# Layer 1 of a masked attention network: edge blocks made by GpSimd in 16-bit words, row of maxima kept in PSUM

## The chip, the cores and the metric

The kernel runs on one core of a Trainium2 chip. The metric is the device time of one execution in microseconds (us), from launch to end. One core has five instruction queues that matter here: TensorE (PE in the profile; its weight loads are PEld), VectorE (DVE), ScalarE (ACT), GpSimd (POOL) and SyncE (SP, which only issues DMAs). They meet at semaphores: an instruction waits until a counter has reached a value, and the queue behind it waits too.

## What is computed

Three attention layers over a graph of 8192 nodes with 64 features, with one dense 0/1 adjacency of 8192 x 8192. In each layer a node i scores each neighbour j with leaky_relu(u_i + v_j), sets non-neighbours to a huge negative number, takes a softmax over j and sums the features h_j by it. Cut to its core:

```
# layer 0
s = (Wh @ a1)[:, None] + (We @ a2)[None, :]
e = where(adj > 0, leaky_relu(s, 0.2), -9e15)
x = layernorm(x + elu(softmax(e, 1) @ entity + x))
# layers 1 and 2, W, L1, L2, attn of their own
e = leaky_relu(u + v.T + c, 0.2)
h = 0.2 * x + 0.8 * elu(softmax(where(adj > 0, e, NEG)) @ (h @ W))
# end
out = layernorm(x + concat([x, h1, h2]) @ mlp_w + mlp_b)
```

## The kernel before

Each layer is done in 16 blocks of 512 rows i (`NB`), and each block in 64 tiles (`NT`) of 128 neighbours j. A tile is 128 x 512: neighbours on the partitions, rows of the block along the free axis. The loops are written out, and the order of the work on each engine is the order in which its function issues it: inside a block a step t from 0 to 63, with side work hung at fixed steps by constants (`T_TURN`, `T_XOR`, `T_HIST` and so on).

One tile goes through four engines. DVE starts the scores (`start_scores`, L1156): max(ua + 0.8 v_j, cb) into one of five PSUM banks `eps`. Here `ua` (row `ub` plus the row maxima) and `cb` (the row of maxima with its sign and factor) are 128 x 512 in SBUF. PE adds the mask into the same bank (L754, two matmuls, each of 64 columns of the array). ACT takes the exponential out of PSUM into `prob` (L577). PE multiplies it with the features into the bank `acc` (L798). A bank of `eps` can be started again only when ACT has read it, five tiles later. In layers 0 and 2 a further bank `den` collects the denominators (L807); in layer 1 one feature channel is replaced so that the sums hold the denominators too, and `den` lies unused. The eighth bank, `misc`, takes all the small work.

The row maxima of block b+1 are found in block b. The adjacency is stored transposed as one byte per edge, 0x38 for "no edge" and 0 for "edge", in the buffer `nt`: two blocks in turn, each in four parts m of 128 x 8192 bytes. `make_edges` (L1004) flips a part into `edges` (two buffers in turn) with an exclusive or on 32-bit words, 128 x 2048. PE counts the edges by level of v_j (`count_edges`, L765: 16 matmuls for each m, four side by side, which land in `misc`). ACT copies the counts out (`counts_out`, L633), PE folds them (`turn_counts`, L774), DVE finds the maximum level and the row value in a chain of small operations (`head`, L1022 to L1048), PE turns them into a row (`turn_maxima`, L841), ACT copies the row out (`maxima_out`, L637), PE spreads it over the partitions into `misc` (`spread_maxima`, L846), ACT copies that to `cb` (`rows_out`, L641), and DVE adds it to `ub` (`add_u`, L1162). In the steps of block b: edges of the four parts at t = 29, 32, 40 and 41 on DVE; counts on PE at t = 35, 35, 43 and 43; fold at 47; head at 51 to 53; turned maxima at 56; spread at 57; `add_u` at 63.

The tail of block b-1 (normalisation, elu, products for the next layer) lies in block b too: sums turned at t = 8, aggregation on DVE at 13, features at 20, products at 27 and 29 on PE, the output sum on DVE at t = 35 (`tail_output`, L1121). GpSimd's queue holds for each block only the tail's DMA issues: it waits for `s_oe` (products copied out) and issues the store of `u` (L521), waits for `s_y` (L1121) and issues the store of `xin` (L524). SP's queue loads the mask parts of block b+1 (`mask_load`, L437); each load waits until PE has used up the same buffer in block b-1, and part 3 thus until block b begins.

Of the kernel before, what the change touches and what calls it, by code (L numbers as in the profile page):

```python
# [16 lines left out]
P = 128  # L17
# [22 lines left out]
EDGE_FLIP = 0x38383838  # L40
LEVELS = float(HB * LV - 2)
# [63 lines left out]
def build(nc, x, adj, ent, W0, a0, W12, lin_w, lin_b, attn, mlp_w, mlp_b, out):  # L105
    with ExitStack() as ctx:
# [92 lines left out]
        miscb = misc[:, :].bitcast(BF16)  # L199
# [30 lines left out]
        s_xor = sem("edges_made")  # L230
        s_oneh = sem("levels_on_columns")
# [73 lines left out]

        def freed(l, b, j):

            if j >= ES:
                return tile(l, b, j) - ES + 1
            last = max(i for i in range(NT) if i % ES == j)  # L310
            return tile(l, b, last) - NT + 1

# [180 lines left out]
        def _(pool):  # L493
# [37 lines left out]
            for l in range(NLAYER):  # L531
                for b in range(NB):
                    tail(l, b)
# [3 lines left out]
        def _(act):  # L537
# [60 lines left out]
            def columns_out(l, b):  # L598
                act.wait_ge(s_htt, blk(l, b) + 1)
                nc.scalar.activation(ht[0:C, :], misc[0:C, :], ACT.Copy).then_inc(s_hte, 1)  # L600

            def products_out(l, b, i):

                act.wait_ge(s_om, 4 * blk(l, b) + i + 1)
                if i < 2:
                    v = misc[:, 0:2 * WC].rearrange("p (r w) -> p r w", w=WC)
# [19 lines left out]
                elif l < 2:  # L626

                    act.wait_ge(s_ust, 16 + 16 * blk(l, b))
                    nc.scalar.activation(urow[:, :], misc[0:RT, 0:P], ACT.Copy).then_inc(s_oe, 2)

            def counts_out(l, b):
                act.wait_ge(s_hist, MV * (blk(l, b) + 1))
                nc.scalar.activation(hs[:, :], misc[:, :], ACT.Copy).then_inc(s_hse, 1)  # L633

            def maxima_out(l, b, par):
                act.wait_ge(s_mt, blk(l, b) + 1)
                nc.scalar.activation(mrow[0:3, par, :], miscb[0:3, 0:BI], ACT.Copy).then_inc(s_mte, 1)  # L637
# [18 lines left out]
            for l in range(NLAYER):  # L656
                counts_out(l, 0)
                maxima_out(l, 0, 0)
                rows_out(l, 0, 0)

                def body(b, par, head, tail):
                    for t in range(NT):
# [8 lines left out]
                        if b == 0 and l == 1 and t == T_FSUM:  # L671
                            act.wait_ge(s_fs1, 1)
                            nc.scalar.activation(acc_s[0:C, 0:P], misc[0:C, 0:P], ACT.Copy).then_inc(s_fs1e, 1)
                        if b == 0 and t == T_FSUM + 4:
                            act.wait_ge(s_fsum, l + 1)
                            nc.scalar.activation(fsum[:, :], misc[:, 0:CE], ACT.Copy).then_inc(s_fsume, 1)
# [4 lines left out]
                        if head and t == T_ROWS:  # L681
# [9 lines left out]
        def _(pe):  # L691
# [66 lines left out]
            def count_edges(l, b, m):  # L758

                n = MV * blk(l, b) + m  # L760
                pe.wait_ge(s_xor, n + 1)
                for k in range(MT // 4):
                    for s in range(4):
                        j = 4 * k + s
                        mm = nc.tensor.matmul(misc[s * HB:(s + 1) * HB, :], oneh[:, m * MT + j, :],  # L765
                                              half_block(edges[:, n % 2, :], m, j), start=(m == 0 and k == 0),
# [4 lines left out]
            def turn_counts(l, b):  # L771
                pe.wait_ge(s_hse, blk(l, b) + 1)
                for r in range(RT):
                    mm = nc.tensor.matmul(misc[:, r * HB:(r + 1) * HB], hs[:, r * P:(r + 1) * P], fold[:, :],  # L774
# [3 lines left out]
            def feature_sum(l, j):  # L778
                if l == 1:
                    mm = nc.tensor.matmul(misc[0:C, 0:P], feat[:, 1, j, 0:C], ones[:, :], start=(j == 0),  # L780
# [4 lines left out]
                mm = nc.tensor.matmul(misc[:, 0:CE], ones[:, :], feat[:, l % 2, j, :], start=(j == 0),  # L785
# [52 lines left out]
            def turn_maxima(l, b):  # L838
                pe.wait_ge(s_split, blk(l, b) + 1)
                for r in range(RT):  # L840
                    mm = nc.tensor.transpose(miscb[0:3, r * P:(r + 1) * P], parts[:, r, 0:3], identb[:, :])  # L841
                mm.then_inc(s_mt, 1)

            def spread_maxima(l, b, par):
                pe.wait_ge(s_mte, blk(l, b) + 1)
                nc.tensor.matmul(misc[:, :], onesb[:, :], mrow[:, par, :], start=True, stop=True).then_inc(s_cb, 1)  # L846

            def tail_step(l, b, t):
                if t == T_TURN:
# [4 lines left out]
                    for r in range(RT):  # L854
                        if l == 1:
                            mm = nc.tensor.matmul(misc[:, r * CE:(r + 1) * CE], acc_s[:, r * P:(r + 1) * P],
                                                  turnw[:, :], start=True, stop=True)
                            continue
                        nc.tensor.matmul(misc[:, r * CE:r * CE + C], acc_s[:, r * P:(r + 1) * P], halves[:, 0:C],  # L859
                                         start=True, stop=True)  # L860
                        mm = nc.tensor.matmul(misc[:, r * CE + C:(r + 1) * CE], den_s[:, r * P:(r + 1) * P],  # L861
                                              halves[:, C:CE], start=True, stop=True)
                    mm.then_inc(s_gt, 1)
                if t == T_HT:
                    for r in range(RT):
                        mm = nc.tensor.transpose(misc[0:C, r * P:(r + 1) * P], hn[:, r, :], ident[:, :])  # L866
# [426 lines left out]
```

## Time and profile before

| what | value |
|---|---|
| median of 3 runs | 3498.52 us (3497.92 to 3498.54) |
| the profiled execution | 3499.27 us, of which the span from first to last instruction is 3497.5 us |
| busy share of the span | PE 92%, DVE 82%, ACT 65%, POOL 3% |
| mean granted TensorE clock | 0.983 |
| layer 0 | to about 1412 us; reads the 268 MB adjacency, DMA share 1.00 |
| layer 1 | about 1412 to 2380 us; 16 blocks, of which 14 in the middle follow each other at 56.9 us |
| layer 2 | about 2440 us to the end |

"Busy" is the time in which at least one instruction of the engine runs; matmul ends are modelled. A timeline row merges neighbours of one kind: start, length of the whole row, engine, line, operation, output<-inputs, shapes and count. "[1.01 <-ACT prob L577]" says that the engine sat idle for 1.01 us before it, until that line of ACT let it go.

### The profile page before, as it was taken

How to read it: one execution, taken by the hardware profiler on the slowest of the kernel's cores; microseconds unless marked ns; L12 is line 12 of the kernel's file. 1: busy time of each engine (PE TensorE's matmuls, PEld its weight loads, DVE VectorE, ACT ScalarE, POOL GpSimd, SP SyncE). 2: the span in 40 equal slices, each digit the busy share in tenths (PEclk: the TensorE clock that was granted, in tenths of full speed). 3: DMA queues.
4: the chain of work that ended last, by engine and by line, in shares of the span. 5: the costliest groups of instructions: out<-in, count | busy, mean ns of one | idle time of the engine just before them, and what ended most of it. 6: DMA issues, size and time to landing. Idle time of an engine off the chain costs nothing. (4 is left out here: it accounts for less than half of the span.)

```text
span 3497.5 us, 58252 instructions
## 1 busy us (share of the span) xinstructions
PE 3203.8 (92%) x22959; PEld 1152.7 (33%) x22959; DVE 2873.2 (82%) x5283; ACT 2269.0 (65%) x3933; POOL 114.3 (3%) x138
## 2 busy tenths in 40 slices
PE   1679999999999999799999999988999999999998
PEld 0323333333333333333333333334333333333333
DVE  5468888888888875699999999986888888888886
ACT  0247766676776666377777787773666666666665
POOL 0000000000000000000000000000000000000000
PEclk9989999999999999899999999998999999999999
DMA  8999999999999951222222222112111211221210
GB/s 253 283 348 346 341 329 347 336 333 340 343 333 341 333 180 54 85 85 97 76 100 73 100 73 101 72 61 85 69 72 64 90 71 57 86 82 57 85 33 7
DMA packets 414116, 578.71 MB, mean 165 GB/s; under 512 B 294402, under 2 KB 315010, under 8 KB 389266
## 3 DMA queue, kind: packets, MB, share of 16 engines
q1 hardware_dynamic: 409458, 564.40, 50.2%
q0 software_dynamic: 4384, 10.59, 1.0%
q8 instruction: 180, 2.95, 0.4%
q14 instruction: 94, 0.77, 0.1%
HBM read 430.10 MB, written 77.69 MB: 145 GB/s over the span
## 5 line engine op out<-in xcount | busy, mean ns | idle before, releaser
L1156 DVE SCALAR_TENSOR_TENSOR eps<-ua,v8col,cb 128x512 f32<-128x512 f32 x2800 | 1971.3, 754 | 376.3 <-ACT prob L577 238.9
L577 ACT ACTIVATE prob<-eps,v2col 128x512 f32<-128x512 f32 x2560 | 1628.4, 688 | 692.2 <-PE eps L754 678.9
L798 PE MATMUL acc<-prob,feat 128*64 128x512 f32 x5120 | 1303.3, 605 | 6.6 <-ACT acc_s L585 6.6
L754 PE MATMUL eps<-nt,nbig 128*64 128x512 fp8e4 (+2 forms) x6542 | 994.3, 384 | 114.4 <-DVE eps L1156 110.4
L754 PEld LDWEIGHTS eps<-nt,nbig 128*64 128x64 bf16 (+2 forms) x6542 | 329.8, 104 | 956.0 <-DVE eps L1156 612.5
L798 PEld LDWEIGHTS acc<-prob,feat 128*64 128x64 f32 x5120 | 326.2, 137 | 397.9 <-issue 215.0
L577 ACT ACTIVATE mi<-eps,v2col 128x512 f32<-128x512 f32 x512 | 328.0, 686 | 156.7 <-PE eps L754 152.7
L995 DVE TENSOR_SCALAR mi<-stage 128x1024 uint8<-128x1024 int32 x512 | 352.2, 689 | 62.9 <-DMA stage<-in_adj_dram 62.5
L807 PE MATMUL den<-prob,ones 128*32 128x512 f32 x3072 | 397.0, 604 | 0.0
L798 PE MATMUL acc<-mi,feat 128*64 128x512 f32 x1024 | 264.8, 597 | 0.0
L1004 DVE TENSOR_SCALAR edges<-nt 128x2048 int32<-128x2048 int32 x192 | 234.2, 1220 | 31.1 <-PE misc L765 16.3
L765 PE MATMUL misc<-edges,oneh 128*32 128x512 fp8e4 x3072 | 190.8, 390 | 70.6 <-DVE edges L1004 55.8
L564 ACT ACTIVATE eps<-ub,v8col 128x512 f32<-128x512 f32 x272 | 189.4, 696 | 0.0
L807 PEld LDWEIGHTS den<-prob,ones 128*32 128x32 f32 x3072 | 67.1, 108 | 301.0 <-issue 301.0
L765 PEld LDWEIGHTS misc<-edges,oneh 128*32 128x32 bf16 x3072 | 85.0, 98 | 198.3 <-issue 81.1
L807 PE MATMUL den<-mi,ones 128*32 128x512 f32 x1024 | 123.1, 598 | 0.0
L751 PE MATMUL eps<-mrow,onesb 128*32 128x512 bf16 (+1 forms) x800 | 106.5, 379 | 0.0
L633 ACT ACTIVATE hs<-misc 128x512 f32<-128x512 f32 x48 | 28.3, 589 | 93.8 <-PE misc L765 93.8
L798 PEld LDWEIGHTS acc<-mi,feat 128*64 128x64 f32 x1024 | 68.2, 137 | 54.4 <-issue 20.2
L878 PEld LDWEIGHTS misc<-wcat,ht 65*128 65x128 f32 x384 | 52.5, 198 | 77.8 <-issue 49.5
L637 ACT ACTIVATE mrow<-misc 3x512 bf16<-3x512 bf16 x48 | 28.1, 586 | 76.3 <-PE misc L841 76.3
L878 PE MATMUL misc<-wcat,ht 65*128 65x130 f32 (+1 forms) x384 | 69.8, 306 | 6.5 <-ACT pj L624 4.5
(159 smaller groups left out, 1407.1 us busy)
## 6 DMA issues: line engine op xcount, KB each, us to landing
stage<-in_adj_dram SPq DMA_DIRECT2D x512, 512.0 KB, 6.5
nt<-nt_d SPq DMA_DIRECT2D x128, 1024.0 KB, 5.2
nt_d<-nt SPq DMA_DIRECT2D x64, 1024.0 KB, 7.2
ub<-u_d SPq DMA_DIRECT2D x48, 256.0 KB, 5.2
xy_d<-xin POOLq DMA_DIRECT2D x32, 256.0 KB, 3.3
xin<-xy_d SPq DMA_DIRECT2D x32, 256.0 KB, 2.9
nt<-mi SPq DMA_TRANSPOSE x256, 7.2
xin<-in_x_dram SPq DMA_DIRECT2D x16, 128.0 KB, 6.3
```

The lines of the kernel that those rows point to most:

```text
L564: nc.scalar.activation(eps[:, j % ES, :], ub[:, par, :], ACT.Relu, bias=v8col[:, j:j + 1], scale=1.0 - ALPHA).then_inc(s_filla, 1)
L577: nc.scalar.activation(weights(l, j), eps[:, j % ES, :], ACT.Exp, bias=v2col[:, j:j + 1]).then_inc(s_p, 1)
L633: nc.scalar.activation(hs[:, :], misc[:, :], ACT.Copy).then_inc(s_hse, 1)
L751: nc.tensor.matmul(et[c:c + cols, :], onesb[:, c:c + cols], mrow[:, par, :], start=False, stop=False, skip_group_check=True, tile_position ...
L754: mm = nc.tensor.matmul(et[c:c + cols, :], nbig[:, c:c + cols], edge, start=False, stop=True, skip_group_check=True, tile_position=(0, c))
L765: mm = nc.tensor.matmul(misc[s * HB:(s + 1) * HB, :], oneh[:, m * MT + j, :], half_block(edges[:, n % 2, :], m, j), start=(m == 0 and k == 0),
L798: mm = nc.tensor.matmul(acc[h:h + C, :], feat[:, l % 2, j, 0:C], weights(l, j), start=(k == 0), stop=(k == NT // 2 - 1))
L807: mm = nc.tensor.matmul(den[32 * i:32 * i + 32, :], ones[:, 0:32], weights(l, QUAD * k + i), start=(k == 0), stop=(k == NT // QUAD - 1))
L878: mm = nc.tensor.matmul(misc[:, r * WC + w:(r + 1) * WC], ht[:, (2 * i + r) * P:(2 * i + r + 1) * P], wcat[:, l, w:WC], start=True, stop=True)
L995: dv.tensor_scalar(out, src, 0, ONE8, ALU.is_le, ALU.mult).then_inc(s_mask, 1)
L1004: dv.tensor_scalar(edges[:, n % 2, :].bitcast(I32), nt[:, b % 2, m, :].bitcast(I32), EDGE_FLIP, None, ALU.bitwise_xor).then_inc(s_xor, 1)
L1156: dv.scalar_tensor_tensor(eps[:, j % ES, :], ua[:, par, :], v8col[:, j:j + 1], cb[:, par, :], ALU.add, ALU.max).then_inc(s_fill, 1)
```

## The change

It touches layer 1 only, in four ways.

- `make_edges` for blocks 1 to 15 of layer 1 leaves DVE's queue and goes to GpSimd's. The 32-bit exclusive or becomes multiply by -1 and add 0x3838 on 16-bit words, in four instructions of 128 x 1024 words for each part m. So GpSimd gets 16 such instructions for each block. Block 0's edges stay on DVE.
- The edge buffers of parts 2 and 3 are new ones, laid over `mi`, which is idle in layer 1 (`edges1`); parts 0 and 1 keep `edges`.
- GpSimd's queue in block b is now: parts 0 and 1 of block b+1, the tail of block b-1 with its two waits and two DMA issues, parts 2 and 3 of block b+1. PE's `count_edges` waits for GpSimd's semaphore `s_edge`.
- In layer 1 the copy of the maxima row to `cb` on ACT (`rows_out`) is gone. The row stays in the PSUM bank where PE spread it, and `start_scores` and `add_u` read it there. `misc` and `den` change roles from block to block: one holds the row of the running block, the other takes the small work.

```diff
+        edges1 = mi[:, :, :].rearrange("p s w -> p (s w)").rearrange("p (m w) -> p m w", m=2)
...
+        def max_bank(b):
+
+            return (misc, den)[b % 2][:, :]
+
+        def work_bank(l, b):
+
+            return max_bank(b + 1) if l == 1 else misc[:, :]
+
+        def by_pool(l, b):
+            return l == 1 and b > 0
+
+        def edge_buffer(l, b, m):
+
+            return edges1[:, m - 2, :] if by_pool(l, b) and m >= 2 else edges[:, m % 2, :]
...
-            for l in range(NLAYER):
-                for b in range(NB):
-                    tail(l, b)
+            def make_edges(b, m):
+
+                n = MV * blk(1, b) + m
+                sl, count = landed(1, b, m)
+                pool.wait_ge(sl, count)
+                if b > 1:
+                    pool.wait_ge(s_hist, n - MV + 1)
+                elif m < 2:
+                    pool.wait_ge(s_hist, n - 1)
+                w = MT * BI // EDGE_PARTS
+                for i in range(EDGE_PARTS):
+                    nc.gpsimd.tensor_scalar(edge_buffer(1, b, m)[:, i * w:(i + 1) * w].bitcast(U16),
+                                            nt[:, b % 2, m, i * w:(i + 1) * w].bitcast(U16), -1.0,
+                                            float(EDGE_FLIP & 0xffff), ALU.mult, ALU.add).then_inc(s_edge, 1)
+
+            for b in range(NB):
+                tail(0, b)
+            for b in range(NB):
+                for m in range(MV if b < NB - 1 else 0):
+                    make_edges(b + 1, m)
+                    if m == 1 and b > 0:
+                        tail(1, b - 1)
+            tail(1, NB - 2)
+            tail(1, NB - 1)
+            for b in range(NB):
+                tail(2, b)
...
-                        if head and t == T_ROWS:
+                        if head and t == T_ROWS and l != 1:
                             rows_out(l, b + 1, 1 - par)
...
-                pe.wait_ge(s_xor, n + 1)
+                if by_pool(l, b):
+                    pe.wait_ge(s_edge, EDGE_PARTS * (MV * (b - 1) + m + 1))
+                else:
+                    pe.wait_ge(s_xor, MV * (NB + 1 + b if l == 2 else blk(l, b)) + m + 1)
...
-                dv.scalar_tensor_tensor(eps[:, j % ES, :], ua[:, par, :], v8col[:, j:j + 1], cb[:, par, :],
+                dv.scalar_tensor_tensor(eps[:, j % ES, :], ua[:, par, :], v8col[:, j:j + 1], maxima(l, b, par),
                                         ALU.add, ALU.max).then_inc(s_fill, 1)
...
-                            for m in range(MV):
+                            for m in range(0 if by_pool(l, b + 1) else MV):
                                 if t == T_XOR[m]:
                                     make_edges(l, b + 1, m)
```

The other edits of the diff replace `misc` by `work_bank(...)` where PE, ACT and DVE use the small-work bank.

## Rows read from the trace of the kernel before

**Rows 1.** Busy time by stretch: one middle block of layer 1, then block 0 of it.

```profile
core 0: us, PE busy (x) PEld busy (x) DVE busy (x) ACT busy (x) POOL busy (x), PEclk, DMA share, GB/s
1899.50:1956.40 56.90, 53.45 (x342) 19.10 (x338) 54.02 (x97) 44.02 (x78) 1.30 (x2) 1.00 0.25 88
1428.80:1501.20 72.40, 68.35 (x417) 31.49 (x419) 53.00 (x83) 41.30 (x66) 0.00 (x0) 0.95 0.13 44
```

**Rows 2.** Who waited for whom in that block: us in total, times, longest.

```profile
PEld eps L754 <- DVE eps L1156: 18.3, 33, 1.7
...
DVE eps L1156 <- ACT prob L577: 2.2, 3, 1.0
```

**Rows 3.** Timeline of DVE through that block.

```profile
1899.49 0.69 DVE L1162 SCALAR_TENSOR_TENSOR ua<-ub,cb 128x512 f32<-128x512 f32 x1
1900.21 9.37 DVE L1156 SCALAR_TENSOR_TENSOR eps<-ua,v8col,cb 128x512 f32<-128x512 f32 x14
...
1926.16 1.22 DVE L1004 TENSOR_SCALAR edges<-nt 128x2048 int32<-128x2048 int32 x1
1927.30 2.07 DVE L1156 SCALAR_TENSOR_TENSOR eps<-ua,v8col,cb 128x512 f32<-128x512 f32 x3
1929.29 0.41 DVE L1121 TENSOR_TENSOR xin<-xin,pj 128x256 f32<-128x256 f32 x1
...
1941.61 0.76 DVE L1156 SCALAR_TENSOR_TENSOR eps<-ua,v8col,cb 128x512 f32<-128x512 f32 x1 [1.01 <-ACT prob L577]
...
1944.19 0.29 DVE L1022 TENSOR_SCALAR he<-misc 128x128 int32<-128x128 int32 x1
...
1948.68 0.17 DVE L1048 CAST parts<-nm 128x4 bf16<-128x4 f32 x1
...
1956.36 0.69 DVE L1162 SCALAR_TENSOR_TENSOR ua<-ub,cb 128x512 f32<-128x512 f32 x1
```

**Rows 4.** Timeline of PE in the same block.

```profile
1930.79 1.91 PE L765 MATMUL misc<-edges,oneh 128*32 128x512 fp8e4 x32
1932.63 0.62 PE L754 MATMUL eps<-nt,nbig 128*64 128x512 fp8e4 x4
...
1933.94 0.60 PE L754 MATMUL eps<-nt,nbig 128*64 128x512 fp8e4 x4
...
1938.54 1.91 PE L765 MATMUL misc<-edges,oneh 128*32 128x512 fp8e4 x32
```

**Rows 5.** Groups of instructions in layer 1, 1480 to 2380 us: count, busy, mean ns, idle before.

```profile
L1071 DVE SCALAR_TENSOR_TENSOR g<-fsum,emp,misc 128x65 f32<-128x65 f32 x64 | 13.6, 275 | 4.9 <-PE misc L856 4.9
...
L641 ACT ACTIVATE cb<-misc 128x512 f32<-128x512 f32 x15 | 9.0, 597 | 7.5 <-PE misc L846 7.5
...
L1022 DVE TENSOR_SCALAR he<-misc 128x128 int32<-128x128 int32 x16 | 4.7, 291 | 4.3 <-PE misc L774 2.9
...
L1024 DVE TENSOR_TENSOR hx<-hx,he 128x128 f32<-128x128 f32 x15 | 4.4, 293 | 0.5
```

**Rows 6.** Timeline of GpSimd in the same block.

```profile
1930.00 0.78 POOL L524 DMA_DIRECT2D xy_d<-xin  x1 [0.44 <-DVE xin L1121]
```

**Rows 7.** All of GpSimd's instructions by form, whole span: busy, mean ns.

```profile
L527 POOL TENSOR_TENSOR rstd<-mom,half 128x4 f32<-128x4 f32 x16 | 23.0, 1435 | 1053.3 <-DVE mom L1060 1053.3
...
L499 POOL MEMSET mrow<- 128x1024 bf16 x1 | 1.0, 951 | 0.1
...
L506 POOL TENSOR_SCALAR_AFFINE_SELECT halves<-halves 128x64 f32<-128x64 f32 x2 | 0.5, 238 | 0.1
...
L502 POOL TENSOR_SCALAR_AFFINE_SELECT identb<-identb 128x128 bf16<-128x128 bf16 x1 | 0.3, 290 | 0.0
...
L499 POOL MEMSET ident<- 128x128 f32 x1 | 0.2, 204 | 0.1
```

**Rows 8.** Timeline of SP's queue in the same block.

```profile
1933.16 24.13 SPq L437 DMA_DIRECT2D nt<-nt_d  x4
```

**Rows 9.** Line 1156 over the whole span: duration ns min/median/max.

```profile
L1156 DVE SCALAR_TENSOR_TENSOR eps<-ua,v8col,cb x2800: 728/754/762, 125.5 to 3469.9; 128x512 f32<-128x512 f32 x187
```

More of the change, by code:

```diff
@@ L230, in build @@
         s_xor = sem("edges_made")
+        s_edge = sem("edges_made_by_pool")
         s_oneh = sem("levels_on_columns")
@@ L599, in columns_out @@
                 act.wait_ge(s_htt, blk(l, b) + 1)
-                nc.scalar.activation(ht[0:C, :], misc[0:C, :], ACT.Copy).then_inc(s_hte, 1)
+                nc.scalar.activation(ht[0:C, :], work_bank(l, b + 1)[0:C, :], ACT.Copy).then_inc(s_hte, 1)
             def products_out(l, b, i):
@@ L764, in count_edges @@
                         j = 4 * k + s
-                        mm = nc.tensor.matmul(misc[s * HB:(s + 1) * HB, :], oneh[:, m * MT + j, :],
-                                              half_block(edges[:, n % 2, :], m, j), start=(m == 0 and k == 0),
+                        mm = nc.tensor.matmul(wb[s * HB:(s + 1) * HB, :], oneh[:, m * MT + j, :],
+                                              half_block(eb, m, j), start=(m == 0 and k == 0),
                                               stop=(m == MV - 1 and k == MT // 4 - 1), skip_group_check=True,
@@ L773, in turn_counts @@
                 for r in range(RT):
-                    mm = nc.tensor.matmul(misc[:, r * HB:(r + 1) * HB], hs[:, r * P:(r + 1) * P], fold[:, :],
+                    mm = nc.tensor.matmul(work_bank(l, b - 1)[:, r * HB:(r + 1) * HB], hs[:, r * P:(r + 1) * P], fold[:, :],
                                           start=True, stop=True)
@@ L779, in feature_sum @@
                 if l == 1:
-                    mm = nc.tensor.matmul(misc[0:C, 0:P], feat[:, 1, j, 0:C], ones[:, :], start=(j == 0),
+                    mm = nc.tensor.matmul(work_bank(1, 0)[0:C, 0:P], feat[:, 1, j, 0:C], ones[:, :], start=(j == 0),
                                           stop=(j == NT - 1))
@@ L784, in feature_sum @@
                     return
-                mm = nc.tensor.matmul(misc[:, 0:CE], ones[:, :], feat[:, l % 2, j, :], start=(j == 0),
+                mm = nc.tensor.matmul(work_bank(l, 0)[:, 0:CE], ones[:, :], feat[:, l % 2, j, :], start=(j == 0),
                                       stop=(j == NT - 1))
@@ L840, in turn_maxima @@
                 for r in range(RT):
-                    mm = nc.tensor.transpose(miscb[0:3, r * P:(r + 1) * P], parts[:, r, 0:3], identb[:, :])
+                    mm = nc.tensor.transpose(work_bank(l, b - 1).bitcast(BF16)[0:3, r * P:(r + 1) * P], parts[:, r, 0:3], identb[:, :])
                 mm.then_inc(s_mt, 1)
@@ L845, in spread_maxima @@
                 pe.wait_ge(s_mte, blk(l, b) + 1)
-                nc.tensor.matmul(misc[:, :], onesb[:, :], mrow[:, par, :], start=True, stop=True).then_inc(s_cb, 1)
+                nc.tensor.matmul(work_bank(l, b - 1), onesb[:, :], mrow[:, par, :], start=True, stop=True).then_inc(s_cb, 1)
             def tail_step(l, b, t):
+                wb = work_bank(l, b + 1)
                 if t == T_TURN:
@@ L877, in tail_step @@
                             w = C if l == 0 else 0
-                            mm = nc.tensor.matmul(misc[:, r * WC + w:(r + 1) * WC],
+                            mm = nc.tensor.matmul(wb[:, r * WC + w:(r + 1) * WC],
                                                   ht[:, (2 * i + r) * P:(2 * i + r + 1) * P], wcat[:, l, w:WC],
@@ L921, in body @@
                         if b == 0 and t < (NT + 2) // 3:
-                            if t == 0:
-                                pe.wait_ge(s_cbe, blk(l, 0) + 1)
+                            if t == 0 and l != 1:
+                                pe.wait_ge(s_cbe, copied(l, 0))
                             for j in range(3 * t, min(3 * t + 3, NT)):
@@ L927, in body @@
                             pe.wait_ge(s_fs1e, 1)
-                            nc.tensor.matmul(misc[:, 0:CE], acc_s[0:C, 0:P], turnw[0:C, :], start=True,
+                            nc.tensor.matmul(work_bank(1, 0)[:, 0:CE], acc_s[0:C, 0:P], turnw[0:C, :], start=True,
                                              stop=True).then_inc(s_fsum, 1)
@@ L1148, in tail_step, with maxima @@
                     tail_result(b)
+            def maxima(l, b, par):
+                return max_bank(b) if l == 1 else cb[:, par, :]
             def start_scores(l, b, j, par):
```

46 lines of the change are left out of this document (27 added, 19 removed).

## The prediction

> **What bounds the kernel now.** The change touches layer 1 alone, so I read that layer and nothing of the whole span. I cut one middle block out of it with the view of busy time by stretch [rows 1]: 56.9 us, DVE busy 54.02 (95%), PE 53.45, ACT 44.02, GpSimd 1.30. Two engines are close to full, so the next question is who waits for whom [rows 2]: in the block PE's weight loads wait 18.3 us for DVE's line 1156, while DVE waits 2.2 us for ACT. DVE sets the pace and PE follows closely behind. The timeline of DVE [rows 3] gives the price of a tile: 14 starts of scores in 9.37 us are (9.37 - 0.75)/13 = 0.663 us from start to start. The timeline of PE [rows 4] gives PE's price where it isn't waiting: 1933.94 - 1932.63 = 1.31 us for two tiles, 0.655 us each. The engines differ by 1% on the plain tile; what side work each has beside its 64 tiles, and where, decides. Block 0 of layer 1 is another case: 72.4 us with PE busy 68.35 and DVE 53.00 [rows 1], bound by PE.
>
> **What leaves DVE.** Four edge instructions for each block. Each takes 1.22 us, and the next start of scores comes 1927.30 - 1926.16 = 1.14 us after it began [rows 3]: 4 x 1.14 = 4.56 us of 56.9. Block 0 loses them too, but there DVE is not the bound, so I count nothing. Blocks 1 to 14 make the edges of the next block: 14 blocks gain at most 14 x 4.56 = 64 us.
>
> **What comes up behind it.** PE's two pairs of counts stand at t = 35 and 43 and take 1932.63 - 1930.79 = 1.84 us each [rows 4]; with the fold at 47, some 0.9 us, PE has about 4.6 us of side work between t = 35 and 47. Until now DVE had its edges in the same stretch and the two cancelled. Afterwards DVE has only the output sum there, 0.3 us (1929.29 to about 1929.6, rows 3 with its three starts before). DVE can run about four tiles ahead on five banks, 4 x 0.66 = 2.6 us. What is left, 4.6 - 0.3 - 2.6 = 1.7 us, becomes a wait of DVE for ACT, where it waits some 1.3 us today (1.01 of it in one place [rows 3]). By DVE's sum a block is 56.9 - 4.56 + 0.4 = 52.7 us. PE's busy time of 53.45 us [rows 1] stands against that; a part of it is modelled matmul tails while it waits, so it is not a hard floor, but I take it as the nearer limit: a gain of 56.9 - 53.45 = 3.4 us.
>
> **The copy of the row that goes.** ACT loses one instruction of 597 ns in each block [rows 5]. ACT is busy 44.02 of 56.9 us [rows 1], so this is worth nothing by itself. The path from the spread row to `add_u` is 0.6 us shorter, but `add_u` stands at the block's last step and shows no idle time before it [rows 3]. Nothing, once 0.6 us at the layer's start. The turn of the two banks costs no instruction: the wait of the small work in the bank of the old row is already met, since that block's last start of scores is eight steps past when t = 8 comes.
>
> **The maxima read from PSUM.** 64 starts for each block now read one operand in PSUM and write PSUM. No row of before shows that pair. The nearest rows [rows 5]: line 1022 reads 128 x 128 from PSUM in 291 ns and line 1024 does as much from SBUF alone in 293 ns; line 1071 reads 65 elements from PSUM beside an SBUF operand in 275 ns. So I take zero. Bounds: minus 0.01 us, and above by line 1071: 275 ns less 65 elements at 1.04 ns leaves 207 ns fixed, against 754 - 533 = 221 ns at line 1156 [rows 9]; these rows give no positive end, and I leave 0.03 us as room, 64 x 0.03 = 1.9 us a block.
>
> A rule speaks against this. The Trainium skill, "VectorE: DVE Perf Modes", section "The TRN2 errata — SBUF-src ops pay a fixed extra latency per instruction", gives VectorE 58 cycles of fixed cost with an SBUF source and 120 with a PSUM source. By it each start would be some 65 ns longer, 4.1 us a block, and the gain would be gone. The rows of 128 x 128 here, 291 against 293 ns, don't agree with it.
>
> **GpSimd's price.** The trace has no GpSimd instruction that streams 1024 words in and out. What it has [rows 7]: a memset of 128 x 1024 in 951 ns and of 128 x 128 in 204 ns, so 747/896 = 0.83 ns for an element; a select with input and output of 128 x 64 in 238 and of 128 x 128 in 290 ns, 0.81 ns for an element and 186 ns fixed. By that slope 1024 words take 186 + 1024 x 0.83 = 1.04 us. Upper bound: two arithmetic operations and the conversion from and to 16 bits could cost a second pass, 0.19 + 2 x 0.85 = 1.9 us (estimate). Lower bound: 0.95 us. The power of 128 x 4 at 1435 ns shows that this engine's software can be far slower than its elements, so the upper end isn't far-fetched. I take 1.0 us from start to start, nearest to the select, which also reads and writes. In all 16 x 1.0 = 16 us of a block of which GpSimd uses 1.3: room enough. The order is what matters.
>
> **The wait that is added.** PE's counts wait for `s_edge`, and behind that wait stands all of PE: masks, products, then ACT and DVE. For parts 0 and 1 there is no danger: their masks are issued in SP's queue from 1933.16 [rows 8], in the block before, and GpSimd makes them right after parts 2 and 3, some 25 us or more before t = 35 of the next block. Parts 2 and 3 are late by construction: GpSimd's queue has the tail before them, which waits for `s_y` (line 1121 on DVE, t = 35), and then issues a DMA of 0.78 us that ends at 1930.78 [rows 6]. PE's first pair of counts starts at 1930.79, the second at 1938.54 [rows 4]: 7.75 us, and part 3 is wanted 0.9 us later. In a shorter block this becomes 1.84 + 8 x 0.655 = 7.1 us, 8.0 us for part 3. Eight instructions of 1.0 us take 8.0 us. It just fits; GpSimd gains a little since DVE reaches t = 35 up to 1 us earlier against PE. I charge 0.4 us a block. The two issues of DMA aren't delayed: parts 0 and 1 have been done long before. The loads of SP depend on PE's masks, as before.
>
> **The sum.** 3.4 - 0.4 = 3.0 us for each of 14 blocks, 42 us. Made against the profiled execution (3499.27 us, span 3497.5) this gives 3457; the median of the runs lies 0.75 us below that execution, so 3456.5 us.
>
> **Rivals.**
>
> A, GpSimd blocks DVE. Parts 0 and 1 of the block after next run right behind parts 2 and 3, from about 8 to 16 us after the first counts. DVE's chain of row maxima lies at 1944.19 to 1948.85, 13.4 to 18 us after them [rows 3, 4], a little earlier in a shorter block: it would run against some four GpSimd instructions. If a GpSimd instruction holds something that the chain's two-operand instructions need, about three of them wait 0.8 us each: 2.4 us, DVE's sum 55.1 us, gain 1.8 x 14 = 25 us, 3473 us. If all four are waited for in full, 4 us, the gain is nearly gone, 3495. For: nothing in the trace. Against: line 1156 has two SBUF operands and never takes more than 762 ns [rows 9], also while GpSimd computes its power in layers 0 and 2, though that touches only 4 elements. The Trainium skill, "SBUF — State Buffer", section "Who interferes with whom", says just this: a VectorE instruction with two SBUF inputs, or in a two-port mode, and a GpSimd instruction that reads SBUF exclude each other for their whole length. By it the starts of scores, with one SBUF input left, would be safe, and the chain would pay.
>
> B, GpSimd is slower than 1.5 us an instruction, and the kernel gets slower. Then PE stands at part 3's wait, at t = 43 of every block. At 1.7 us part 3 is late by 8 x 1.7 - 8.0 = 5.6 us, and DVE's sum is 52.7 + 5.6 = 58.3 us, 1.4 more than now: 14 x 1.4 = 20 us, 3518 us. It decides from 8T - 8.0 = 4.2, T = 1.53 us. At the upper bound of 1.9 us it would be 3540 us. For: no row of such an instruction, and the 1435 ns. Against: the slope of 0.8 ns for an element with input and output.
>
> C, a start of scores costs more with PSUM on both sides. DVE's sum has 56.9 - 52.7 = 4.2 us to lose, so from 4.2/64 = 0.066 us for each start the gain is gone: 3498 us, no change, and slower beyond. Against: the 291 ns row.
>
> D, the edges come off DVE and the time stays, because PE's chain is the true bound at today's pace. Against: PE waits 18.3 us for DVE in a block [rows 2]. Within 0.2%.
>
> **How the numbers follow.** Chances: the sum 0.45; A 0.22 (0.04 of it no change); B 0.22 (0.18 slower, 0.04 no change); C 0.07 (half no change, half slower); D 0.04. Differences below 0.2%, 7 us, can't be told from none. So faster 0.63, no change 0.15, slower 0.22. Low end: DVE's full 4.56 us for 14 blocks gives 3435. High end: B at 1.7 us, 3518, with what lies above it left out.
>
> **What would show it.** The block in layer 1 should be 53.9 us, against 52.7 by DVE alone. GpSimd's edge instructions 1.0 to 1.05 us. Line 1156 at 754 ns and 0.663 us from start to start; 0.73 would be C. PE's idle time at the counts should be under 1 us a block in place of the waits for line 1156; several us there, released by GpSimd, are B. Lines 1022 to 1048 on DVE should still take 4.7 us from first to last; 7 us or more, or instructions of 0.3 us that take 1 us, are A. Layers 0 and 2 should keep their lengths to 1 us. Wrong above all would be the one price that no row carries: that of a GpSimd instruction on 1024 16-bit words.

## The result

The changed kernel takes 3533.7 us (median of 5 executions, 3518.0 to 3534.5), the kernel before 3497.9 us beside it; the ratio is 1.009, interval 1.0078 to 1.0103. It is slower by 36 us, where 42 us less were forecast. The profiled execution took 3534.2 us, with a span of 3532.3 us.

The page of the changed kernel, busy time and two groups of GpSimd (busy, mean ns, idle before):

```profile
PE 3203.6 (91%) x22848; PEld 1160.9 (33%) x22959; DVE 2839.7 (80%) x5223; ACT 2265.7 (64%) x3917; POOL 366.1 (10%) x378
...
L563 POOL TENSOR_SCALAR edges<-nt 128x1024 uint16<-128x1024 uint16 x120 | 125.6, 1047 | 64.0 <-PE den L814 41.4
...
L563 POOL TENSOR_SCALAR mi<-nt 128x1024 uint16<-128x1024 uint16 x120 | 125.5, 1046 | 9.5
```

GpSimd went from 3% to 10% of the span, DVE from 2873.2 to 2839.7 us: 60 edge instructions are gone, 73 us, but more than half of that has come back, most of it (some 29 us) in the chain of row maxima, as the rows below show. The clock differs from execution to execution: the four of 3529.8 to 3534.5 us ran at a mean granted clock of 0.974 to 0.976, the one of 3518.0 us at 0.983, as before the change.

A block of layer 1 from `add_u` to `add_u` was 56.87 us [rows 3]. Of the same 14 blocks the first 13 now take between 58.6 and 60.5 us, mostly 59.1 and 60.2 us in turn, 59.55 us on average; the 14th takes 57.1 us. The timeline of one of them on DVE, with waits:

```profile
1980.51 0.68 DVE L1219 SCALAR_TENSOR_TENSOR ua<-ub,den 128x512 f32<-128x512 f32 x1
...
2008.69 0.76 DVE L1210 SCALAR_TENSOR_TENSOR eps<-ua,v8col,den 128x512 f32<-128x512 f32 x1 [0.67 <-ACT prob L621]
...
2014.90 5.37 DVE L1210 SCALAR_TENSOR_TENSOR eps<-ua,v8col,den 128x512 f32<-128x512 f32 x8 [1.83 <-ACT prob L621]
2022.42 0.75 DVE L1210 SCALAR_TENSOR_TENSOR eps<-ua,v8col,den 128x512 f32<-128x512 f32 x1 [2.15 <-ACT prob L621]
...
2025.01 0.29 DVE L1072 TENSOR_SCALAR he<-misc 128x128 int32<-128x128 int32 x1
2025.34 0.60 DVE L1073 SCALAR_TENSOR_TENSOR hx<-he,kstep 128x128 f32<-128x128 int32 x1
2025.97 1.09 DVE L1074 TENSOR_TENSOR hx<-hx,he 128x128 f32<-128x128 f32 x1
2027.09 0.29 DVE L1075 TENSOR_REDUCE kmax<-hx 128x4 f32<-128x128 f32 x1
2027.41 0.66 DVE L1076 TENSOR_SCALAR emp<-kmax 128x4 f32<-128x4 f32 x1
2027.98 0.28 DVE L1077 TENSOR_SCALAR vm<-kmax,gst 128x4 f32<-128x4 f32 x1
2028.29 0.89 DVE L1080 SCALAR_TENSOR_TENSOR ns<-vm,gst,vucol 128x4 f32<-128x4 f32 x1
...
2031.74 0.17 DVE L1098 CAST parts<-nm 128x4 bf16<-128x4 f32 x1
...
2039.71 0.68 DVE L1219 SCALAR_TENSOR_TENSOR ua<-ub,misc 128x512 f32<-128x512 f32 x1
```

Three things stand in it. The four edge instructions are gone, and in their place DVE waits for ACT: 0.67, 1.83 and 2.15 us are the longest waits. The chain of row maxima, which began 44.7 us into the block [rows 3], begins after 44.5 us: 4.56 us of work have left DVE's queue and the chain has come 0.2 us forward. And the chain itself, 4.66 us from line 1022 to 1048 [rows 3], takes 6.9 us: its small instructions of 0.17 to 0.3 us take 0.60, 1.09, 0.66 and 0.89 us. GpSimd beside it:

```profile
2010.38 0.78 POOL L545 DMA_DIRECT2D xy_d<-xin  x1
2011.24 8.93 POOL L563 TENSOR_SCALAR mi<-nt 128x1024 uint16<-128x1024 uint16 x8
2020.24 8.93 POOL L563 TENSOR_SCALAR edges<-nt 128x1024 uint16<-128x1024 uint16 x8
```

It works without a pause from 2011.24 to 2029.17, and the last instruction of the chain that is long starts at 2028.29. Everything after that has its old length. Not all of the long ones have two operands in SBUF: line 1076, with one SBUF input and a constant, takes 0.66 us in place of 0.17, while line 1077, with one SBUF input and two scalars read from SBUF, keeps its 0.28 us. The same block by stretch, first the kernel before and then the changed one: to the first counts, to the chain, the chain, to the next `add_u`.

```profile
core 0: us, PE busy (x) PEld busy (x) DVE busy (x) ACT busy (x) POOL busy (x), PEclk, DMA share, GB/s
1899.50:1930.80 31.30, 29.50 (x169) 10.58 (x166) 31.13 (x54) 26.75 (x50) 1.30 (x2) 1.00 0.13 43
1930.80:1944.20 13.40, 13.14 (x123) 5.32 (x122) 11.99 (x18) 8.34 (x14) 0.00 (x0) 1.00 0.59 208
1944.20:1948.80 4.60, 3.47 (x20) 1.14 (x20) 4.19 (x17) 3.21 (x5) 0.00 (x0) 1.00 0.46 194
1948.80:1956.40 7.60, 7.34 (x41) 2.06 (x37) 6.72 (x12) 5.71 (x10) 0.00 (x0) 1.00 0.00 0
```

```profile
1980.50:2011.80 31.30, 29.87 (x169) 10.97 (x165) 29.85 (x54) 27.23 (x50) 1.91 (x3) 1.00 0.12 44
2011.80:2025.00 13.20, 12.98 (x123) 5.32 (x122) 8.80 (x13) 8.37 (x14) 12.25 (x13) 1.00 0.58 209
2025.00:2031.90 6.90, 3.52 (x18) 1.06 (x18) 6.48 (x17) 3.22 (x5) 3.94 (x4) 0.97 0.32 132
2031.90:2039.70 7.80, 7.64 (x34) 2.42 (x33) 6.68 (x11) 4.95 (x8) 0.00 (x0) 0.81 0.00 1
```

The first two stretches have nearly kept their length although DVE does 1.3 and 3.2 us less in them: PE is busy 13.14 of 13.4 us and 12.98 of 13.2 us in the second. The third is 2.3 us longer. The fourth, in which nothing was added and a copy was taken from ACT, is 0.2 us longer too, and there the granted clock is 0.81 in place of 1.00.

The changed kernel holds a control of its own: the 14th block. GpSimd has made the last edges before its chain begins. Its chain and the stretch behind it:

```profile
2323.41:2328.05 4.64, 3.52 (x20) 1.13 (x20) 4.22 (x17) 3.22 (x5) 0.00 (x0) 1.00 0.00 0
2328.05:2334.67 6.62, 6.21 (x32) 1.79 (x31) 6.58 (x11) 4.97 (x8) 0.00 (x0) 1.00 0.00 0
```

Without GpSimd beside it the chain takes 4.64 us again, and the clock stays at 1.00.

PE's timeline shows where the clock can have fallen; it pauses 2.72 us, then 0.66 us, while DVE is in the chain:

```profile
2026.67 1.03 PE L847 MATMUL acc<-prob,feat 128*64 128x512 f32 x4
2030.42 0.41 PE L799 MATMUL eps<-nt,nbig 128*64 128x512 fp8e4 x2 [2.72 <-DVE eps L1210]
2031.49 0.64 PE L799 MATMUL eps<-nt,nbig 128*64 128x512 fp8e4 x2 [0.66 <-DVE eps L1210]
2031.91 1.91 PE L847 MATMUL acc<-prob,feat 128*64 128x512 f32 x4
```

The next four products take 1.91 us in place of 1.03.

From these I formed theory H: the edges were hidden behind PE; what costs is that GpSimd excludes DVE's two-operand instructions, and that PE's pause during the chain lets its clock fall. The words "two-operand" are too narrow: line 1076 has one.

### The profile page after: what moved, and what is told of

It is laid out like the page before. It is cut to its first block and busy times, and to the rows that moved or that the text cites. A ratio compares the mean times of both kernels' runs of the same rounds, so it can differ in the third digit from the quotient of the medians.

```text
span 3532.3 us, 58303 instructions
## 1 busy us (share of the span) xinstructions
PE 3203.6 (91%) x22848; PEld 1160.9 (33%) x22959; DVE 2839.7 (80%) x5223; ACT 2265.7 (64%) x3917; POOL 366.1 (10%) x378
## 5 line engine op out<-in xcount | busy, mean ns | idle before, releaser
L1210 DVE SCALAR_TENSOR_TENSOR eps<-ua,v8col,cb 128x512 f32<-128x512 f32 x1776 | 1269.7, 755 | 323.6 <-ACT prob L621 188.5
L847 PE MATMUL acc<-prob,feat 128*64 128x512 f32 x5120 | 1320.6, 612 | 7.0 <-ACT acc_s L629 7.0
L1210 DVE SCALAR_TENSOR_TENSOR eps<-ua,v8col,misc 128x512 f32<-128x512 f32 x512 | 349.8, 751 | 72.4 <-ACT prob L621 71.3
L1210 DVE SCALAR_TENSOR_TENSOR eps<-ua,v8col,den 128x512 f32<-128x512 f32 x512 | 347.7, 750 | 50.0 <-ACT prob L621 49.1
L814 PE MATMUL misc<-edges,oneh 128*32 128x512 fp8e4 x2336 | 147.6, 395 | 71.2 <-DVE edges L1054 56.3
L1054 DVE TENSOR_SCALAR edges<-nt 128x2048 int32<-128x2048 int32 x132 | 161.2, 1221 | 30.5 <-PE misc L814 16.6
L538 POOL TENSOR_TENSOR rstd<-mom,half 128x4 f32<-128x4 f32 x16 | 23.1, 1446 | 1096.3 <-DVE mom L1110 1096.3
L563 POOL TENSOR_SCALAR edges<-nt 128x1024 uint16<-128x1024 uint16 x120 | 125.6, 1047 | 64.0 <-PE den L814 41.4
L548 POOL TENSOR_TENSOR rstd<-mom,half 128x4 f32<-128x4 f32 x16 | 23.0, 1438 | 1051.0 <-DVE mom L1110 1051.0
L563 POOL TENSOR_SCALAR mi<-nt 128x1024 uint16<-128x1024 uint16 x120 | 125.5, 1046 | 9.5
L814 PEld LDWEIGHTS misc<-edges,oneh 128*32 128x32 bf16 x2336 | 67.7, 99 | 166.1 <-issue 64.2
```

Source lines behind the costliest of these rows:

```text
L563: nc.gpsimd.tensor_scalar(edge_buffer(1, b, m)[:, i * w:(i + 1) * w].bitcast(U16), nt[:, b % 2, m, i * w:(i + 1) * w].bitcast(U16), -1.0, ...
L814: mm = nc.tensor.matmul(wb[s * HB:(s + 1) * HB, :], oneh[:, m * MT + j, :], half_block(eb, m, j), start=(m == 0 and k == 0), stop=(m == MV ...
L847: mm = nc.tensor.matmul(acc[h:h + C, :], feat[:, l % 2, j, 0:C], weights(l, j), start=(k == 0), stop=(k == NT // 2 - 1))
L1054: dv.tensor_scalar(edge_buffer(l, b, m).bitcast(I32), nt[:, b % 2, m, :].bitcast(I32), EDGE_FLIP, None, ALU.bitwise_xor).then_inc(s_xor, 1)
L1210: dv.scalar_tensor_tensor(eps[:, j % ES, :], ua[:, par, :], v8col[:, j:j + 1], maxima(l, b, par), ALU.add, ALU.max).then_inc(s_fill, 1)
```

## The experiments

Ratios are against the kernel before on the same chip. A block is one in the middle of layer 1. The diffs show the edit that matters, not always all of it. Layer 0 is the same in all kernels, and yet the first `add_u` of layer 1 lies between 1428.6 and 1440.2 us in the profiled executions, so the length of a block is the surer measure.

**The edges off DVE, nothing in their place.**

```diff
-                            for m in range(MV):
+                            for m in range(0 if l == 1 else MV):
                                 if t == T_XOR[m]:
                                     make_edges(l, b + 1, m)
...
```

The constant buffer that PE counts is filled once by GpSimd.

> The kernel before, with DVE's 60 edge instructions of blocks 1 to 15 of layer 1 left out and nothing put in their place: PE counts a constant buffer, so the row maxima are those over all nodes and part of layer 1's result is not the reference's. Theory P (the prediction's step: the edges stand on DVE's path): a block of 53.5 us in place of 56.9, the kernel at 3440 to 3457 us. Theory H (the edges lay in a stretch, t = 24 to 47, that PE bounds anyway, and were hidden behind it): a block of 56.4 to 56.7 us, the kernel at 3490 to 3496 us, and DVE idle for some 4 us more in each block, released by ACT.

Measured: 3492.9 us, ratio 0.9983 (0.9973 to 0.9992), a block of 56.23 us, a little under the range of theory H, which holds against P. DVE's waits in the kernel without edges:

```profile
1933.34 5.40 DVE L1166 SCALAR_TENSOR_TENSOR eps<-ua,v8col,cb 128x512 f32<-128x512 f32 x8 [1.75 <-ACT prob L583]
1940.46 0.76 DVE L1166 SCALAR_TENSOR_TENSOR eps<-ua,v8col,cb 128x512 f32<-128x512 f32 x1 [1.72 <-ACT prob L583]
...
1955.20 0.68 DVE L1172 SCALAR_TENSOR_TENSOR ua<-ub,cb 128x512 f32<-128x512 f32 x1
```

DVE waits 5.7 us in this block in place of 2.2 [rows 2]: of the 4.56 us, 3.5 became waits for ACT, which waits for PE, 0.64 became gain, and the remaining 0.4 us is not accounted for. Fourteen blocks would gain 9 us; the median shows 6.3 us, with an interval from 3 to 9.

**The row in PSUM, edges on DVE.**

```diff
         def by_pool(l, b):
-            return l == 1 and b > 0
+            return False
...
```

GpSimd's queue and PE's wait for the edges are put back as they were before the change.

> The changed kernel with the edges back on DVE: what is left of the change is the row of maxima in PSUM and the two banks in turn. If the PSUM operand is free, 3496 to 3499 us, with line 1156's successor at 750 to 755 ns. If it costs 65 ns for each start of scores, a block of 59 us or more and 3530 us or more, which by itself would be the whole loss of the changed kernel.

Measured: 3484.9 us, ratio 0.9960 (0.9945 to 0.9975), a block of 55.91 us. The operand is free, and more: this half of the change gains 0.96 us a block, and the expectation had nothing of that. ACT's timeline of the kernel before, at the block's end, and the groups of starts in the new kernel:

```profile
1952.16 0.59 ACT L637 ACTIVATE mrow<-misc 3x512 bf16<-3x512 bf16 x1 [0.80 <-PE misc L841]
...
1953.82 0.60 ACT L641 ACTIVATE cb<-misc 128x512 f32<-128x512 f32 x1 [0.50 <-PE misc L846]
1954.31 3.57 ACT L577 ACTIVATE prob<-eps,v2col 128x512 f32<-128x512 f32 x6
```

```profile
L1205 DVE SCALAR_TENSOR_TENSOR eps<-ua,v8col,den 128x512 f32<-128x512 f32 x512 | 347.4, 748 | 12.6 <-ACT prob L616 11.8
L1205 DVE SCALAR_TENSOR_TENSOR eps<-ua,v8col,misc 128x512 f32<-128x512 f32 x470 | 319.7, 750 | 12.7 <-ACT prob L616 11.9
```

Before, two copies of 0.6 us stood close together on ACT, and the exponentials behind them came late to DVE: in the block of [rows 3], DVE's starts wait 0.88 us for ACT at 1955.03. Without the second copy that wait is gone, and the stretch from the chain to `add_u` takes 6.62 us in place of 7.51. ACT was busy 44 of 56.9 us [rows 1] and still late at that one place. The starts take 748 and 750 ns with one operand in PSUM, 754 before [rows 9].

**GpSimd waits for the chain.**

```diff
                 pool.wait_ge(sl, count)
+                if m == 0:
+                    pool.wait_ge(s_split, blk(1, b - 1) + 1)
```

> The changed kernel with one wait more on GpSimd: part 0 of the next block's edges is not begun before DVE's chain of row maxima is done. Theory H with exclusion (GpSimd blocks the chain's two-operand instructions, 2.2 us a block, and PE's pause there lets its clock fall): the chain back from 6.9 to 4.7 us, no stretches at half clock, a block of 56.6 to 57.0 us, 3494 to 3500 us. Rival L (part 3 late at PE, 0.3 us, and the late counts cost the time): unchanged, 3515 to 3535 us.

Measured: 3481.4 us, ratio 0.9948 (0.9933 to 0.9962), a block of 55.75 us. One wait more on GpSimd turns a loss of 36 us into a gain of 18 us. It is even better than expected, by about what the row in PSUM brings. The chain's stretch and the one behind it:

```profile
1934.10:1938.70 4.60, 3.47 (x20) 1.13 (x20) 4.18 (x17) 3.22 (x5) 0.00 (x0) 1.00 0.47 196
1938.70:1945.40 6.70, 6.29 (x36) 1.82 (x35) 6.67 (x12) 4.96 (x8) 6.11 (x6) 1.00 0.00 0
```

The chain takes 4.6 us again and the clock stays at 1.00. GpSimd works now in the fourth stretch, 6.11 of 6.7 us, where DVE has only starts with one SBUF operand and `add_u`.

**A quarter of the counting.**

```diff
-                for k in range(MT // 4):
+                for k in range(1 if l == 1 and b > 0 else MT // 4):
```

> The kernel before, with edges on DVE, but PE does a quarter of the counting matmuls in blocks 1 to 15 of layer 1 (16 of 64 for each block), so part of layer 1's result is not the reference's. It takes 2.8 us of PE's work out of each block's stretch t = 35 to 47. Theory H (PE bounds that stretch): now DVE's edges come to the front; 1 to 2.5 us a block less, 3465 to 3485 us. Theory P (DVE bounds it): 0 to 0.3 us a block, 3493 to 3498 us.

Measured: 3479.9 us, ratio 0.9945 (0.9930 to 0.9959), a block of 55.57 us. It is the counterpart of the first experiment: in the same stretch 2.8 us less on PE gain 1.3 us a block, while 4.56 us less on DVE gained 0.64. PE was the nearer bound there, and DVE's edges were close behind.

**The row back in SBUF, edges on GpSimd.**

```diff
-                return max_bank(b) if l == 1 else cb[:, par, :]
+                return cb[:, par, :]
```

with the copy on ACT and its waits put back.

> The changed kernel with the row of maxima copied to SBUF and read there by the starts of scores, so that these have two SBUF operands again; GpSimd still makes the edges. Theory X (a GpSimd instruction and a VectorE instruction with two SBUF operands exclude each other): starts beside GpSimd's 16 instructions wait for up to 1 us each, some 10 to 16 us a block, the kernel at 3650 to 3780 us, with starts of scores of 1.5 us and more in the trace. Rival (only the chain's small instructions suffer): 3545 to 3555 us, that is the changed kernel plus the 14 us of the copy.

Measured: 3614.0 us, ratio 1.0331 (1.0310 to 1.0352), a block of 64.85 us. DVE beside GpSimd's work:

```profile
1984.90 3.40 DVE L1209 SCALAR_TENSOR_TENSOR eps<-ua,v8col,cb 128x512 f32<-128x512 f32 x5
...
1991.82 5.02 DVE L1209 SCALAR_TENSOR_TENSOR eps<-ua,v8col,cb 128x512 f32<-128x512 f32 x5
1997.03 15.67 DVE L1209 SCALAR_TENSOR_TENSOR eps<-ua,v8col,cb 128x512 f32<-128x512 f32 x11 [0.19 <-ACT prob L621]
```

Eleven starts take 15.67 us, 1.42 us each in place of 0.66: each waits for the GpSimd instruction that runs, and GpSimd for each start (its mean went from 1.05 to 1.28 and 1.37 us). So theory X holds in kind. I had expected 3650 to 3780 us, too much; that the starts that run at this pace are fewer and that a part of the delay falls where PE bounds is my guess. Against the 3534 us with the row in PSUM the difference is 80 us, of which the copy on ACT is some 13. What the copy costs without GpSimd beside it shows in the 14th block, where GpSimd has no edges left: the chain takes 4.65 us and the stretch behind it 7.51 us, as before the change, against 6.62 without the copy.

**One piece for each part.**

```diff
-EDGE_PARTS = 4
+EDGE_PARTS = 1
```

> The changed kernel with each edge part made in one GpSimd instruction of 4096 words in place of four of 1024. By theory X what counts is how long GpSimd still works when the chain begins, 44.5 us into the block, and how many gaps it leaves: one instruction takes some 3.6 us, four of them end about 45.5 us into the block, so the chain waits once, about 0.7 us, and then runs free; part 3 is in time. Block 56.0 to 56.5 us, clock without falls, kernel at 3480 to 3492 us. Rival (a longer instruction holds DVE longer, so the loss grows): 3535 us and more.

Measured: 3520.2 us, ratio 1.0063 (1.0043 to 1.0083), blocks of 57.4 to 58.8 us. Neither expectation. The chain waits once, as foreseen (a block of 57.81 us):

```profile
2017.46 0.29 DVE L1072 TENSOR_SCALAR he<-misc 128x128 int32<-128x128 int32 x1
2017.79 1.55 DVE L1073 SCALAR_TENSOR_TENSOR hx<-he,kstep 128x128 f32<-128x128 int32 x1
2019.38 0.29 DVE L1074 TENSOR_TENSOR hx<-hx,he 128x128 f32<-128x128 f32 x1
```

but for 1.3 us and not 0.7: GpSimd's four instructions take 3.6 us each, the third waits 0.54 us here for its load (from 0 to 2.1 us in others), so they end 45.8 us into the block, and the chain begins at 44.1, not 44.5. And the clock does fall, to 0.80 behind the chain, so that a delay of 1.3 us costs 2.5 us against the best kernel below. Longer instructions bring less loss here: the harm doesn't grow with the length of one instruction.

**Eight pieces for each part.**

```diff
-EDGE_PARTS = 4
+EDGE_PARTS = 8
```

> The changed kernel with each edge part in eight GpSimd instructions of 512 words. By the slope 0.70 us from start to start, 11.2 us for parts 2 and 3 in place of 8.9: part 3 is some 2.5 us late at PE, and GpSimd still works through the whole chain, so more of its instructions wait, each for less (0.3 us on average, some nine of them). Block 61 to 63 us, kernel at 3555 to 3590 us. Rival (short instructions hold DVE little, so the loss shrinks): below 3520 us.

Measured: 3557.8 us, ratio 1.0171 (1.0150 to 1.0191), blocks of 60.9 and 62.0 us. The mean of a GpSimd instruction is 0.62 us, part 3 comes late, the fold at 47.2 us in place of 43.4, and more instructions of the chain are stretched, each by less (line 1074 by 0.3 us, 1080 by 0.2, 1085 and 1093 by 0.3). The chain itself is shorter than in the changed kernel, 5.9 to 6.0 us in nearly all blocks; what makes these blocks longer is that it begins 48.3 us into them and not 44.5. So smaller pieces cost here through the late part 3, not through the chain.

**Everything before the tail.**

```diff
                 pool.wait_ge(sl, count)
+                if m == 0:
+                    pool.wait_ge(s_split, blk(1, b - 1) + 1)
+                if m == 2 and b > 1:
+                    pool.wait_ge(s_h, blk(1, b - 1))
...
-                    if m == 1 and b > 0:
+                    if m == 3 and b > 0:
                         tail(1, b - 1)
```

> The changed kernel with GpSimd's order changed: parts 0 and 1 only when the chain of row maxima is done, parts 2 and 3 only when DVE has finished the features of the tail (t = 20), and all four before the tail's two DMA issues. So GpSimd works beside no two-operand instruction of DVE and no part is late. Expected: the gain of the row in PSUM (0.96 us a block) and of the edges (0.64 us) together, a block of 55.3 us, the kernel at 3469 to 3476 us. If the gain of the two doesn't add up: 3478 to 3485 us, as with the wait for the chain alone.

Measured: 3475.4 us, ratio 0.9936 (0.9920 to 0.9953), a block of 55.36 us: the fastest kernel of the study, 23 us under the one before. GpSimd's timeline:

```profile
1960.81 8.93 POOL L567 TENSOR_SCALAR mi<-nt 128x1024 uint16<-128x1024 uint16 x8 [15.39 <-issue]
1972.26 0.56 POOL L542 DMA_DIRECT2D u_d<-urow  x1 [2.52 <-ACT urow L677]
...
1991.86 8.92 POOL L567 TENSOR_SCALAR edges<-nt 128x1024 uint16<-128x1024 uint16 x8 [18.25 <-DVE parts L1102]
```

Parts 2 and 3 end 2.5 us before the tail's store has to go out. The two gains add up: 0.96 + 0.64 = 1.60 us, and 56.87 - 55.36 = 1.51 us. Against the wait for the chain alone, 55.75 - 55.36 = 0.39 us is what the late part 3 cost.

**The chain made longer, without GpSimd beside it.**

```diff
+                for i in range(7 if by_pool(l, b) else 0):
+                    step(dv.tensor_reduce(kmax[:, :], hx[:, :, :], AX, ALU.max), s_delay, 7 * (b - 1) + i + 1)
                 step(dv.tensor_reduce(kmax[:, :], hx[:, :, :], AX, ALU.max), s_headseq, at + 4)
```

> The kernel of the run before the tail (3475 us, no instruction beside which GpSimd works is blocked) with seven reductions more in DVE's chain of row maxima in each block of layer 1, some 2.3 us, as much as GpSimd's blocking adds to the chain of the changed kernel. Theory C (the length of the chain alone does all the harm: 2.3 us directly, and PE's pause lets its clock fall behind the chain, 1.1 us more): block 58.5 to 59 us with granted clock about 0.8 behind the chain, 3520 to 3530 us; in executions without the clock's fall 3508 to 3512. Rival G (GpSimd's work itself costs more than the chain's delay): block 57.6 us, no fall of the clock, 3508 to 3512 us in all.

Measured: 3527.6 us, ratio 1.0080 (1.0060 to 1.0101), blocks of 58.2 to 59.8 us, 58.8 us on average. The chain and the stretch behind it, in a block of 58.8 us:

```profile
1958.50:1965.40 6.90, 3.53 (x20) 1.14 (x20) 6.24 (x24) 3.22 (x5) 0.00 (x0) 1.00 0.30 127
1965.40:1973.20 7.80, 7.80 (x34) 2.10 (x32) 6.67 (x11) 4.95 (x8) 7.18 (x7) 0.78 0.00 0
```

Two stretches of 6.9 and 7.8 us, to the tenth those shown above for the changed kernel, and a clock of 0.78, with no GpSimd instruction beside the chain. The delay of the chain alone makes the whole picture, the clock's fall too. Over all blocks the clock behind the chain is 0.70 to 0.87 here and 0.71 to 0.87 in the changed kernel. The chain is 2.24 us longer than in the kernel of 3475.4 us and the block 3.4 us, so 1.2 us a block is the clock's.

**The same with three reductions.**

> The same with three reductions more, some 1.0 us. Theory C: the direct part only or a part of the fall, since PE's pause is shorter: block 56.3 to 57.4 us, 3489 to 3505 us. If the delay were hidden in part (DVE idles 5 us a block elsewhere): under 56 us, 3480 us.

Measured: 3490.7 us, ratio 0.9976 (0.9964 to 0.9987), a block of 56.31 us. A chain longer by 0.96 us costs 0.95 us, and the clock stays at 1.00 in all blocks. But the length of the delay alone doesn't decide whether the clock falls. The chain and the stretch behind it, first here, then in a block of the kernel with one piece for each part:

```profile
1769.27:1774.87 5.60, 3.53 (x20) 1.14 (x20) 5.08 (x20) 3.22 (x5) 0.00 (x0) 1.00 0.40 167
1774.87:1781.49 6.62, 6.37 (x33) 1.79 (x31) 6.58 (x10) 4.96 (x8) 6.07 (x6) 1.00 0.00 0
```

```profile
1785.30:1790.75 5.45, 3.52 (x20) 1.14 (x20) 5.04 (x17) 3.22 (x5) 1.29 (x1) 1.00 0.36 150
1790.75:1798.56 7.81, 7.81 (x33) 2.11 (x31) 6.68 (x10) 4.95 (x8) 0.00 (x0) 0.78 0.00 0
```

The shorter chain has the fall, to 0.78, and the longer one has not. With eight pieces, where chains take 5.9 to 6.6 us, the clock behind the chain fell in three of 13 blocks only, to 0.83. What decides between the two is open.

**The changed kernel again.**

> The changed kernel once more, unaltered, for the spread of its executions beside the mean granted clock of each. Theory C: executions with a mean clock of 0.983 take some 3518 us, those with 0.975 some 3534 us, nothing in between that the clock doesn't follow. Rival: times between 3518 and 3534 us at one and the same clock.

Measured: 3534.1 us, ratio 1.0095 (1.0078 to 1.0112), four executions: 3529.8 and 3531.9 us at a clock of 0.976, 3536.2 at 0.974 and 3537.0 at 0.973. Time follows clock. An execution of 3518 us at 0.983 did not come again, so that end rests on one.

## Why the prediction was wrong

Two steps failed: the gain that the sum took for the edges, 3.4 us a block where 0.64 came, and the delay of DVE's chain by GpSimd, which the sum had at nothing and left to rival A, where it measured 2.25 us a block and brought a fall of the clock with it.

The sum of what the runs show, for a block: 56.87 us before; minus 0.64 for the edges, minus 0.96 for the copy on ACT, plus 0.39 for the late part 3, plus 2.25 for the chain: 57.9 us, against 59.55 measured on average in the 13 blocks. What is left, 1.6 us, I put down to the clock; in the run with the longer chain alone the clock's part was 1.2 us. In 13 blocks these are 16 to 21 of the 36 us; the one execution of 3518 us at a clock of 0.983, against 3534, gives 16.

- **What leaves DVE, and what comes up behind it** (4.56 us, and 3.4 us gained after PE). This step failed. The measured 0.64 us are a fifth of the 3.4. I set PE's busy time of the whole block, 53.45 us, against DVE's sum, and added only 0.4 us of new waits. But a block has two kinds of stretches: behind the chain and at the tail's start PE waits for DVE, and from about t = 25 to the chain PE works without a gap. Of the 18.3 us of waits for DVE that I took as proof, 10.5 lie before the first edge instruction and 4.7 in the chain and behind it; the stretch with the four edges, 1923.0 to 1944.2 us, has 3.1 of them, and PE is busy in 20.9 of its 21.2 us. The lead of four tiles that I let DVE gain there is no time won: it is lost when the chain waits for the fold, and the fold waits for PE. The one number to look at was the start of the chain, and what released it. Rival D, at 0.04, came nearest to this term, and the same 18.3 us were held against it.
- **The copy that goes** (nothing). This failed too, on the good side: 0.96 us a block. I looked at ACT's busy share and at `add_u`, and not at the 0.88 us that DVE waits for ACT two starts before it, at 1955.03:

```profile
1955.03 1.42 DVE L1156 SCALAR_TENSOR_TENSOR eps<-ua,v8col,cb 128x512 f32<-128x512 f32 x2 [0.88 <-ACT prob L577]
```

- **The maxima read from PSUM** (zero). Right: 750 ns. The rows of 128 x 128 were the better guide. The Trainium skill, "VectorE: DVE Perf Modes", section "The TRN2 errata — SBUF-src ops pay a fixed extra latency per instruction", would have 65 ns more, by the estimate of the prediction; the trace here doesn't agree with that. Its table is for results written to SBUF, and these starts write PSUM.
- **GpSimd's price** (1.04 us, 1.0 from start to start). Right in the first, 1047 ns; from start to start it is (8.93 - 1.05)/7 = 1.13 us. I had taken the distance below the duration, as the selects have it, and there is a gap of 0.08 us instead. Rival B, which needed 1.53 us, fell with it.
- **The wait that is added** (0.4 us for part 3). Right in the number, 0.39 us, and in part by luck: the eight instructions took 8.9 us and not 8.0, but GpSimd began them at 2011.24, 0.6 us before PE's first counts, where the sum had it begin with them.
- **Rival A.** This was the mechanism, at 0.22. Its price was right, 2.4 us forecast and 2.25 measured, though four instructions wait, by 0.3 to 0.8 us, and not three by 0.8; its total, 3473 us, was wrong, because it stood on the 3.4 us of the first step. With 0.64 in its place, A alone gives 56.87 - 0.64 + 0.4 + 2.4 = 59.0 us a block and a slower kernel. I held against it that line 1156 never took more than 762 ns beside GpSimd; that row shows a GpSimd instruction of 4 elements and could not speak about one of 1024. The Trainium skill, "SBUF — State Buffer", section "Who interferes with whom", states the exclusion, and the runs agree: 0.29 to 1.09 us at line 1074, 0.66 to 1.42 us from start to start with two SBUF operands, no change with one, none for the reduction at line 1075. Line 1076, 0.17 to 0.66 us with one SBUF input, fits the words "or in a two-port mode" of rival A; that it ran in such a mode no trace shows, and why line 1077 was spared is open.
- **The clock** was no part of the sum. In the changed kernel PE pauses 2.72 us during the chain and then 0.66 us, against 0.47 and 0.66 us in the kernel of 3475.4 us, and the granted clock of the next stretch is 0.81, that is partly at 1.2 GHz in place of 2.4. The Trainium skill, "TensorE: Matmul & The Clock Gate", section "HAM oscillation — how this bites in real kernels", describes such a fall at every repetition of a pause. The trace agrees: it comes in each of the 13 blocks (0.71 to 0.87 behind the chain), and not in the 14th (1.00).

## What to carry to other kernels

Before you take work off the engine with the larger busy share, find the stretch in which that work lies and ask what releases the next common point behind it; busy sums over a block don't tell, and in one stretch the other engine may be the bound. When an engine's work moves to GpSimd, look at which of DVE's instructions will run beside it: here those with two SBUF operands were held up, and one with a single SBUF input too, while starts with one operand in SBUF and one in PSUM were not. A single wait that moved GpSimd's work past a chain of small instructions made the difference between 36 us lost and 18 us gained. And a copy on an engine that is idle a quarter of the time can still stand in the one place where it is late.

## What was not expected of the hardware

- GpSimd's multiply and add on 128 x 1024 16-bit words: 1.05 us, on 512 words 0.62 us, on 4096 words 3.61 us; that is 0.83 ns a word and about 0.2 us fixed.
- GpSimd and DVE take turns: beside 16 GpSimd instructions a start with two SBUF operands took up to 1.53 us, and GpSimd's own 1.28 and 1.37 us on average in place of 1.05.
- One of DVE's instructions with a single SBUF input, 128 x 4 with a constant, was held up too: 0.66 us in place of 0.17.
- A pause of PE longer by 1.0 us in each block left the clock at 1.00; with 2.2 us more it fell in every block, to 0.70 to 0.87 behind the pause, which costs 1.2 us a block beyond the delay itself. With one piece for each part it fell in 13 blocks, in one of them with only 0.8 us more.
